# Moving the turned one-hots of a graph attention from VectorE to ScalarE, with the logit sums earlier in TensorE's turn

## The chip, the cores and the metric

The kernel runs on one core of a Trainium2 chip. The metric is the device time of one execution in microseconds; less is better.

## The reference

Four graph layers run one after another on 6250 nodes with 256 features and 100000 edges sorted by destination. The first is two rounds of graph attention with 8 heads; only this part is touched. One round, cut to what matters:

```python
xs = (x @ Ws).reshape(N, H, C)
alpha = a_i[dst] + a_j[src] + edge_terms            # one logit per edge and head
alpha = jnp.where(alpha >= 0, alpha, 0.2 * alpha)
m = jax.ops.segment_max(alpha, dst, num_segments=N)
e = jnp.exp(alpha - m[dst])
s = jax.ops.segment_sum(e, dst, num_segments=N)
msg = xs[src] * (e / (s[dst] + 1e-16))[:, :, None]
out = jax.ops.segment_sum(msg, dst, num_segments=N)
```

## The kernel before

Edges are cut into 832 slots of 128 edges; each slot belongs to one tile of 127 nodes plus a carried row. `phase_attention` runs once for each of the two attention rounds. It handles the slots in 104 groups of 8, one group to a **turn**; four groups stand unrolled in the body of a hardware loop (SETS = 4), so the two rounds make 208 turns. Every engine has its own in-order program, and semaphores tie them together.

What one group g needs, in the order of its data:

- POOL gathers the 8 blocks of 128 source rows (`gather`, line 609) into one of four buffers `x`. The buffer is free when all pair sums of group g-4 are done (line 605).
- SyncE loads `place`, the edges' node positions spread to all partitions, as bf16 (line 624), and `flag` (line 627).
- **The turned one-hot** `fullT` (128 nodes x 8x128 edges, fp32): a 1 where an edge's position equals the partition's number. In the kernel before VectorE makes it with one comparison (`onehotT`, line 826). There is one buffer, so it waits for the logit sums of the group before.
- TensorE's `logit_sums` (lines 660 to 664): edge terms, then 8 small products with `fullT`, then the gathered logits, all into `psA`. ScalarE copies the result to `z` (`copy_logits`, line 751), VectorE makes `al` of it (`leaky`, line 840), TensorE turns `al` (`turn_logits`, line 671), VectorE runs two scans for the running maximum (`scans`, lines 849 and 850), TensorE turns that back (`turn_max`, line 677), VectorE subtracts it (`shifts`, lines 858 and 859), and ScalarE takes the exponentials (`exps`, lines 758 to 760).
- VectorE multiplies the gathered rows by the exponentials, two slots at a time (`messages`, line 866). TensorE sums them by destination with `main`, the unturned one-hot (`pair_sums`, line 684, four pairs of slots, into four PSUM banks `psO`; `main` is made by VectorE's `onehot`, line 831). ScalarE copies the carried row of each slot (`copy_row`, line 765), and VectorE adds the slot's sum to the node table `agg` (`add`, line 875). An add waits for the row's copy; a pair of sums waits for the adds that free its two banks, those of the pair two before it.
- ScalarE also picks the edge terms of group g+3, eight small copies (`pick_terms`, line 742), and copies the gather's indices (`index`, line 732).
- `keep_busy` (line 689) is two matmuls of 512 columns whose result nobody reads.

The order within a turn g is written out by hand on each engine:

```
TensorE: fills, turn_logits(g+1), pair 0, fills, pair 1, fills, turn_max(g+1), pair 2,
         logit_sums(g+2), fills, pair 3
VectorE: leaky(g+1), messages 0, adds 4 5 of g-1, messages 2, adds 6 7 of g-1, scans(g+1),
         tile numbers of g, onehotT(g+2), messages 4, adds 0 1, messages 6, shifts(g+1),
         adds 2 3, onehot(g+1)
ScalarE: pick_terms(g+3), rows 0 to 3, index(g+4), exps(g+1), rows 4 5, copy_logits(g+2), rows 6 7
```

"Tile numbers" (`tiles_of`) are eight register loads on the engine's sequencer; the adds take their address from them.

Of the kernel before, what the change touches and what calls it, by code (L numbers as in the profile page):

```python
# [16 lines left out]
ALU = mybir.AluOpType  # L17
# [507 lines left out]
def phase_attention(nc, m, d, l, sem):  # L525
# [7 lines left out]
    terms_picked = sem("slot_terms_picked")  # L533
    full_ready = sem("onehotT_ready")
# [21 lines left out]
    with ExitStack() as ctx:  # L556
# [9 lines left out]
        row0 = [sb(f"row0{b}", [1, GROUP, AGG]) for b in range(2)]  # L566
        z = sb("z", [P, GROUP, H])
# [31 lines left out]
        with nc.Block() as block:  # L599
# [19 lines left out]
            @block.sync  # L619
            def _(sp):  # L620
                def load_places(g, b):

                    sp.wait_ge(full_ready, g + 1)
                    sp.dma_start(place[b % 2][:], d.places[bass.ds(g * GROUP, GROUP), :].rearrange("(o s) p -> o (s p)", o=1).to_broadcast([P, GROUP * P])).then_inc(loc_ready[b % 2], 16)

                    sp.wait_ge(mT_ready, g + 1)
                    sp.dma_start(flag[b % 2][:, 0:P], d.flags[bass.ds(g * GROUP, GROUP), :, :].rearrange("s h p -> (s h) p")).then_inc(flag_ready[b % 2], 16)

                def store_rows(g, b):
                    sp.wait_ge(copied, g * GROUP + GROUP + BANKS)  # L630
                    sp.dma_start(d.carry[bass.ds(g * GROUP, GROUP), :].rearrange("(o j) k -> o (j k)", o=1),
                                 row0[b][:].rearrange("o j k -> o (j k)")).then_inc(row_stored[b], 16)
                sp.dma_start(terms[:], d.terms[l - 1]).then_inc(terms_ready, 16)
                sp.wait_ge(zeroed, 2)
                for b in range(2):
                    load_places(b, b)
                for b in range(2):
                    load_places(b + 2, b)
                with sp.Fori(0, NG // 2 - 2) as it:
                    for b in range(2):  # L640
                        load_places(it * 2 + b + 4, b)
                        store_rows(it * 2 + b, b)
                for b in range(4):
                    store_rows(NG - 4 + b, b % 2)
                for b in range(2):
                    sp.wait_ge(row_stored[b], 16 * (NG // 2 + 1))

            @block.tensor
            def _(pe):
                regs = [pe.alloc_register(f"pe_n{l}_{j}") for j in range(GROUP)]  # L650
                pe.wait_ge(zeroed, 4)
# [44 lines left out]
                def group(g, b, turn):  # L696
                    g1, b1 = g + 1, (b + 1) % SETS
                    keep_busy()
                    if exists(g1):
                        turn_logits(g1, b1)  # L700
                    pair_sums(g, b, 0)
                    keep_busy()
                    pair_sums(g, b, 1)
                    keep_busy()
                    if exists(g1):
                        turn_max(g1, b1)
                    pair_sums(g, b, 2)
                    if exists(g + 2):
                        logit_sums(g + 2, (b + 2) % SETS, turn + (b + 2) // SETS)
                    keep_busy()  # L710
                    pair_sums(g, b, 3)
# [3 lines left out]
            def _(act):  # L715
                act.sem_inc(copied, BANKS)
                for b in range(2):
                    act.sem_inc(row_stored[b], 16)
# [26 lines left out]

                def copy_logits(g, b):
# [19 lines left out]

                for g in range(2):
                    ts = tiles_of(g)
                    pick_terms(g, g, ts, range(GROUP))
                act.sem_inc(z_ready, 1)  # L770
                copy_logits(0, 0)
                exps(0, 0)
# [4 lines left out]
                def group(g, b, turn):  # L777
                    if exists(g + 3):
# [8 lines left out]
                    if exists(g + SETS):  # L787
                        index(g + SETS, b, turn + 1)
                    if exists(g + 1):
                        exps(g + 1, (b + 1) % SETS)  # L790
                    copy_row(g, b, 4)
                    copy_row(g, b, 5)
                    if exists(g + 2):
                        copy_logits(g + 2, (b + 2) % SETS)
                    copy_row(g, b, 6)
                    copy_row(g, b, 7)
# [6 lines left out]
            def _(dve):  # L803
                regs = [dve.alloc_register(f"dve_n{l}_{j}") for j in range(GROUP)]
                for b in range(2):
# [4 lines left out]
                dve.sem_inc(full_ready, 2)  # L810
# [9 lines left out]

                def onehotT(g, b, pair):
                    dve.wait_ge(loc_ready[b % 2], pair * 16 + 16)

                    if not (isinstance(g, int) and g == 0):
                        dve.wait_ge(ai_ready, g)
                    nc.vector.tensor_scalar(fullT[:].rearrange("p j e -> p (j e)"), place[b % 2][:], m.pidx[:, 0:1], None, ALU.is_equal).then_inc(full_ready, 1)
# [50 lines left out]
                def period(g, b, turn):  # L877
# [12 lines left out]
                    if last_added:  # L890
                        add(g - 1, b0, 6, ns)
                        add(g - 1, b0, 7, ns)
                    if exists(g1):
                        scans(g1, b1, turn * 2 + (b + 1) // 2)
                    ns = tiles_of(g)
                    if exists(g + 2):
                        onehotT(g + 2, b + 2, turn * 2 + (b + 2) // 2)
# [11 lines left out]
                onehotT(0, 0, 0)  # L909
# [4 lines left out]
                onehotT(1, 1, 0)  # L914
# [1819 lines left out]
```

## Time and profile before

| | |
|---|---|
| median of 3 runs | 8941.31 us (8940.38 to 8955.18) |
| the profiled execution | 8943.65 us, span 8942.0 us |
| mean granted TensorE clock | 0.747 of full speed |
| TensorE matmul busy | 6288.6 us (70%) |
| VectorE busy | 4789.7 us (54%) |
| ScalarE busy | 1926.0 us (22%) |
| POOL busy | 4599.6 us (51%) |
| logits copied to `z` (line 751) | 208 times, 104 a round, from 570.8 us to 3616.4 us |

Busy time doesn't count register, branch and semaphore instructions. "PE" is TensorE's matmuls, "PEld" its weight loads, which overlap them; "DVE" is VectorE and "ACT" ScalarE. A matmul in fp32 stands as two instructions in the trace, so one pair of sums is four. The granted clock is a share of full speed: 1.00 is 2.4 GHz and 0.50 is 1.2 GHz. An idle time "<-issue" is one for which the trace shows no semaphore.

### The profile page before, as it was taken

The page shows a single profiled execution, that of the slowest core. Times are in us where ns is not written, and L with a number is a line of the kernel's source. Part 1 is how long each engine was busy: PE and PEld are TensorE (multiplying, and loading weights), DVE is VectorE, ACT ScalarE, POOL GpSimd, SP SyncE. Part 2 cuts the span into 40 slices and gives each one's busy share as a digit, 9 for nine tenths or more (in the row PEclk, how much of TensorE's full clock was granted, in tenths as well). Part 3 has the DMA queues.
Part 4 walks back from the last instruction along what each step waited for, and adds up shares of the span by engine and source line. Part 5 has one row for each costly group of instructions (what it writes and reads, how often), then busy time and mean ns, then how long its engine had stood idle before and what let it go on. Part 6 is the DMA issues. An engine that isn't in the chain of part 4 may idle for free. (4 is left out here: it accounts for less than half of the span.)

```text
span 8942.0 us, 114148 instructions
## 1 busy us (share of the span) xinstructions
PE 6288.6 (70%) x23568; PEld 4316.3 (48%) x23569; DVE 4789.7 (54%) x9732; ACT 1926.0 (22%) x6808; POOL 4599.6 (51%) x4186
## 2 busy tenths in 40 slices
PE   4548899967789999676777778955555666666650
PEld 2236666635566666355666644434444443443330
DVE  4337766666566767675444431134444644444438
ACT  0223333312333333121000011100000222222221
POOL 0036666610466666004777710047777288888880
PEclk7668887777888878675555559977777788888885
DMA  1384444311444434122111123333333366666665
GB/s 38 106 216 112 112 111 111 107 46 56 149 110 112 110 108 115 36 66 62 31 31 30 31 61 133 135 107 104 104 104 104 79 68 68 68 68 68 68 68 175
DMA packets 578153, 801.90 MB, mean 90 GB/s; under 512 B 100092, under 2 KB 453709, under 8 KB 576718
## 3 DMA queue, kind: packets, MB, share of 16 engines
q0 software_dynamic: 269760, 484.09, 27.2%
q1 hardware_dynamic: 281230, 290.19, 10.8%
q10 hardware_dynamic: 27092, 26.85, 1.2%
q8 instruction: 24, 0.39, 0.0%
q14 instruction: 47, 0.39, 0.0%
HBM read 545.48 MB, written 255.28 MB: 90 GB/s over the span
## 5 line engine op out<-in xcount | busy, mean ns | idle before, releaser
L609 POOL DMA_INDIRECT at_x<-table,at_idx x1664 | 1626.2, 977 | 1976.2 <-ACT at_idx L726 1009.1
L2279 POOL DMA_INDIRECT acc<-sc_rows,sc_idx x832 | 1353.3, 1627 | 298.4 <-DMA acc<-sc_rows,sc_idx 185.0
L684 PE MATMUL at_psO<-at_x,at_main 128*128 128x273 f32 x3328 | 1136.7, 471 | 244.9 <-DVE agg L875 240.2
L1679 POOL DMA_INDIRECT rel_x<-rel_table,rel_idx x832 | 793.0, 953 | 963.2 <-DVE rel_sums L1760 710.0
L1679 POOL DMA_INDIRECT conv_x<-conv_table,conv_idx x832 | 808.4, 972 | 767.0 <-DVE conv_msg L1763 513.7
L684 PEld LDWEIGHTS at_psO<-at_x,at_main 128*128 128x128 f32 x3328 | 709.0, 225 | 536.3 <-issue 378.6
L1732 PE MATMUL rel_psO<-rel_x,rel_hot 128*128 128x256 f32 x1664 | 607.6, 544 | 466.6 <-DMA rel_x<-rel_table,rel_idx 394.5
L2319 PE MATMUL sc_psR<-gated,sc_pick 128*128 x1664 | 593.9, 454 | 455.0 <-ACTq L2357 451.2
L875 DVE TENSOR_TENSOR agg<-agg,at_psO 128x273 f32 x1664 | 725.4, 436 | 246.1 <-DVE agg L875 166.5
L1732 PEld LDWEIGHTS rel_psO<-rel_x,rel_hot 128*128 128x128 f32 x1664 | 463.5, 285 | 611.1 <-issue 471.6
L765 ACT COPY at_row<-at_psO 1x273 f32<-1x273 f32 x1664 | 543.0, 374 | 599.7 <-PE at_psO L684 593.5
L2319 PEld LDWEIGHTS sc_psR<-gated,sc_pick 128*128 128x128 f32 x1664 | 297.9, 211 | 750.1 <-issue 741.1
L1797 DVE TENSOR_TENSOR rel_sums<-rel_sums,rel_psO 128x256 f32 x832 | 349.8, 420 | 503.4 <-PE rel_psO L1732 405.6
L689 PE MATMUL at_psK<-at_keep_x,at_keep_w 128*128 128x512 bf16 x1664 | 609.7, 454 | 0.0
L1732 PE MATMUL conv_psO<-conv_msg,conv_hot 128*128 128x65 f32 x1664 | 381.7, 421 | 309.8 <-DVE conv_msg L1786 293.6
L866 DVE TENSOR_TENSOR at_x<-at_x,at_psE 128x512 f32<-128x512 f32 x832 | 566.1, 681 | 1.6 <-issue 1.6
L2355 ACT COPY sc_rows<-sc_psR 128x257 f32<-128x257 f32 x832 | 311.2, 374 | 1114.8 <-POOLq L2278 1090.0
L662 PE MATMUL at_psA<-a_ij,at_fullT 128*128 x3328 | 534.9, 297 | 0.0
L662 PEld LDWEIGHTS at_psA<-a_ij,at_fullT 128*128 128x128 f32 x3328 | 529.1, 249 | 0.0
L1732 PEld LDWEIGHTS conv_psO<-conv_msg,conv_hot 128*128 128x128 f32 x1664 | 362.7, 330 | 328.7 <-issue 328.7
L2422 DVE SCALAR_TENSOR_TENSOR sc_idxf<-sc_count,sc_delta 128x8 f32<-128x8 f32 x105 | 17.6, 167 | 709.2 <-POOLq L2278 708.8
L1716 PE MATMUL conv_psF<-w_radial,conv_attr 12*128 12x64 f32 x1664 | 381.8, 419 | 20.2 <-DMA conv_attr<-in_attr_T 20.2
(412 smaller groups left out, 9192.8 us busy)
## 6 DMA issues: line engine op xcount, KB each, us to landing
at_place<-places SPq DMA_DIRECT2D x208, 256.0 KB
rel_table<-rt_rows SPq DMA_DIRECT2D x50, 1024.0 KB
at_x<-table,at_idx POOLq DMA_INDIRECT x1664
acc<-zeros ACTq DMA_DIRECT2D x4, 6553.5 KB, 63.1
la_t<-acc SPq DMA_DIRECT2D x40, 642.5 KB
conv_attr<-in_attr_T SPq DMA_DIRECT2D x832, 6.0 KB
conv_x<-conv_table,conv_idx POOLq DMA_INDIRECT x832
rel_x<-rel_table,rel_idx POOLq DMA_INDIRECT x832, 2.8
```

What stands on the lines that cost most here:

```text
L609: pool.indirect_dma_start(x[b][:, j, 0:TABW], None, d.table[0:NR, :], bass.IndirectOffsetOnAxis(ap=idx[b][:, j:j + 1], axis=0)).then_inc(x ...
L662: nc.tensor.matmul(psA[:, j, :], fullT[:, j, :], m.a_ij[:, bass.ds(ns[j] * (2 * H) + H, H)], start=False, stop=False, skip_group_check=True)
L684: ins = nc.tensor.matmul(psO[j % BANKS][:, 0:AGG], main[b % 2][:, j, :], x[b][:, j, 0:AGG], start=True, stop=True)
L689: nc.tensor.matmul(psK[:], keep_w[:], keep_x[:], start=True, stop=True)
L765: nc.scalar.copy(row0[b % 2][:, j, :], psO[j % BANKS][0:1, 0:AGG]).then_inc(copied, 1)
L866: nc.vector.tensor_tensor(v, v, psE[:, j:j + 2, :].unsqueeze(3).to_broadcast([P, 2, H, C]), ALU.mult).then_inc(rhs_ready, 1)
L875: nc.vector.tensor_tensor(to, to, psO[j % BANKS][:, 0:AGG], ALU.add).then_inc(acc_done, 1)
L1679: pool.indirect_dma_start(x[b][:, j, 0:WIDE], None, table, bass.IndirectOffsetOnAxis(ap=idx[b][:, j:j + 1], axis=0)).then_inc(x_ready[b], 16)
L1716: ins = nc.tensor.matmul(psF[b % 2][:, j, :], attr[b % 2][:, j, :], m.w_radial[:], start=True, stop=True)
L1732: ins = nc.tensor.matmul(psO[q][j % PER // (PER // 2)][:, j % (PER // 2), :], hot[b % 2][:, j, :], rhs[:, j, :], start=True, stop=True)
L2279: pool.indirect_dma_start(d.acc[k][0:NR + P, :], bass.IndirectOffsetOnAxis(ap=idx[b][:, j:j + 1], axis=0), rows[b % 2][:, j, :], None, com ...
L2319: nc.tensor.matmul(psR[j % 4][:, 0:K], pick[b % 2][:, j, :], m.gated[:, bass.ds(ns[j] * K, K)], start=True, stop=True).then_inc(r_ready, 1)
```

## The change

`onehotT` moves from VectorE to ScalarE, at the head of its turn, and becomes two activations: the distance |place - p| in bf16 (`away`), then relu(1 - distance) into `fullT`. A wait on a semaphore stands between them. `own` holds -p for each partition and is made once per round. On ScalarE `copy_logits(g+2)` moves ahead of `exps(g+1)`, and rows 4 to 7 follow in one piece. On TensorE `turn_logits` moves ahead of the first fills, `logit_sums(g+2)` moves from behind pair 2 to behind pair 1, and one of the four calls of `keep_busy` goes, so that six fills are left of eight. On VectorE the tile numbers are read before the scans instead of behind them.

```diff
 # TensorE
                 def group(g, b, turn):
                     g1, b1 = g + 1, (b + 1) % SETS
-                    keep_busy()
                     if exists(g1):
                         turn_logits(g1, b1)
+                    keep_busy()
                     pair_sums(g, b, 0)
                     keep_busy()
                     pair_sums(g, b, 1)
-                    keep_busy()
+                    if exists(g + 2):
+                        logit_sums(g + 2, (b + 2) % SETS, turn + (b + 2) // SETS)
                     if exists(g1):
                         turn_max(g1, b1)
                     pair_sums(g, b, 2)
-                    if exists(g + 2):
-                        logit_sums(g + 2, (b + 2) % SETS, turn + (b + 2) // SETS)
                     keep_busy()
                     pair_sums(g, b, 3)
 # ScalarE
+                def onehotT(g, b, pair):
+                    act.wait_ge(loc_ready[b % 2], pair * 16 + 16)
+                    nc.scalar.activation(away[:], place[b % 2][:], ACT.Abs, bias=own[:, 0:1]).then_inc(away_ready, 1)
+                    act.wait_ge(away_ready, g + 1)
+
+                    if not (isinstance(g, int) and g == 0):
+                        act.wait_ge(ai_ready, g)
+                    nc.scalar.activation(fullT[:].rearrange("p j e -> p (j e)"), away[:], ACT.Relu, bias=m.ones[:, 0:1], scale=-1.0).then_inc(full_ready, 1)
...
+                act.wait_ge(zeroed, 1)
+                onehotT(0, 0, 0)
...
                 copy_logits(0, 0)
+                onehotT(1, 1, 0)
                 exps(0, 0)
...
                 def group(g, b, turn):
+                    if exists(g + 2):
+                        onehotT(g + 2, b + 2, turn * 2 + (b + 2) // 2)
                     if exists(g + 3):
                         ts = tiles_of(g + 3)
...
                     if exists(g + SETS):
                         index(g + SETS, b, turn + 1)
+                    if exists(g + 2):
+                        copy_logits(g + 2, (b + 2) % SETS)
                     if exists(g + 1):
                         exps(g + 1, (b + 1) % SETS)
-                    copy_row(g, b, 4)
-                    copy_row(g, b, 5)
-                    if exists(g + 2):
-                        copy_logits(g + 2, (b + 2) % SETS)
-                    copy_row(g, b, 6)
-                    copy_row(g, b, 7)
+                    for j in range(4, GROUP):
+                        copy_row(g, b, j)
 # VectorE
+                nc.vector.tensor_scalar(own[:], m.pidx[:], -1.0, None, ALU.mult).then_inc(zeroed, 1)
...
-                def onehotT(g, b, pair):
-                    dve.wait_ge(loc_ready[b % 2], pair * 16 + 16)
-
-                    if not (isinstance(g, int) and g == 0):
-                        dve.wait_ge(ai_ready, g)
-                    nc.vector.tensor_scalar(fullT[:].rearrange("p j e -> p (j e)"), place[b % 2][:], m.pidx[:, 0:1], None, ALU.is_equal).then_inc(full_ready, 1)
...
                         add(g - 1, b0, 7, ns)
+                    ns = tiles_of(g)
                     if exists(g1):
                         scans(g1, b1, turn * 2 + (b + 1) // 2)
-                    ns = tiles_of(g)
-                    if exists(g + 2):
-                        onehotT(g + 2, b + 2, turn * 2 + (b + 2) // 2)
                     messages(g, b, 4)
```

The first marks of `full_ready` come from ScalarE instead of VectorE, and SyncE and TensorE wait for one more mark of `zeroed`.

## Rows read from the trace of the kernel before

**Rows 1.** Busy time by window: the attention phase, one full-clock stretch, one half-clock stretch.
```profile
...
core 0: us, PE busy (x) PEld busy (x) DVE busy (x) ACT busy (x) POOL busy (x), PEclk, DMA share, GB/s
600.00:1650.00 1050.00, 946.66 (x4033) 657.92 (x4034) 735.12 (x1598) 409.77 (x1764) 657.87 (x673) 0.81 0.41 111
1056.00:1067.00 11.00, 9.29 (x48) 6.24 (x48) 8.59 (x20) 4.82 (x21) 8.44 (x9) 1.00 0.51 136
1068.00:1078.00 10.00, 10.00 (x34) 7.45 (x34) 5.32 (x13) 2.46 (x11) 4.13 (x5) 0.50 0.28 80
...
```

**Rows 2.** Waits from 600 to 1650 us: engine, line, cause, total, times, longest.
```profile
...
DVE at_al L840 <- ACT at_z L751: 163.9, 84, 3.8
...
PE at_psO L684 <- DVE agg L875: 101.6, 90, 2.0
...
```

**Rows 3.** Instruction groups from 600 to 1650 us: busy us, mean ns, idle before.
```profile
...
L609 POOL DMA_INDIRECT at_x<-table,at_idx x673 | 658.0, 978 | 392.4 <-issue 200.7 <-PE at_psO L684 191.6
...
L765 ACT COPY at_row<-at_psO 1x273 f32<-1x273 f32 x672 | 219.4, 374 | 233.6 <-PE at_psO L684 231.6
...
L742 ACT COPY at_slot_terms<-at_terms 128x8 f32 x672 | 125.9, 197 | 36.5 <-issue 35.1
...
```

**Rows 4.** Timeline of a full-clock turn: start us, duration us, engine, line, operation.
```profile
...
1056.35 1.18 PE L684 MATMUL at_psO<-at_x,at_main 128*128 128x273 f32 x4 [1.46 <-DVE agg L875]
...
1057.51 0.41 PE L660 MATMUL at_psA<-at_slot_terms,ident 128*128 128x64 f32 x2
...
1058.00 1.22 DVE L831 TENSOR_TENSOR at_main<-at_psT,loc_m 128x1024 f32<-128x1024 f32 x1
...
1059.76 0.59 PE L689 MATMUL at_psK<-at_keep_x,at_keep_w 128*128 128x512 bf16 x2
...
1060.21 0.22 DVE L840 SCALAR_TENSOR_TENSOR at_al<-at_z 128x64 f32<-128x64 f32 x1 [0.99 <-ACT at_z L751]
1060.35 0.68 DVE L866 TENSOR_TENSOR at_x<-at_x,at_psE 128x512 f32<-128x512 f32 x1
...
1060.95 0.43 DVE L875 TENSOR_TENSOR agg<-agg,at_psO 128x273 f32 x1
...
1061.59 0.44 DVE L875 TENSOR_TENSOR agg<-agg,at_psO 128x273 f32 x1 [0.21 <-DVE agg L875]
...
1063.54 0.41 DVE L849 TENSOR_TENSOR_SCAN at_fwd<-at_flag,at_psT 64x128 f32<-64x128 f32 x1
...
1064.68 1.12 POOL L609 DMA_INDIRECT at_x<-table,at_idx  x1 [0.30 <-issue]
...
1064.93 0.75 DVE L826 TENSOR_SCALAR at_fullT<-at_place,pidx 128x1024 f32<-128x1024 bf16 x1 [0.54 <-issue]
...
1065.60 0.68 DVE L866 TENSOR_TENSOR at_x<-at_x,at_psE 128x512 f32<-128x512 f32 x1
...
1067.41 1.90 PE L684 MATMUL at_psO<-at_x,at_main 128*128 128x273 f32 x4 [1.68 <-DVE agg L875]
...
```

**Rows 5.** Timeline of TensorE in the half-clock turn that follows.
```profile
...
1069.10 0.53 PE L660 MATMUL at_psA<-at_slot_terms,ident 128*128 128x64 f32 x2
...
1073.27 1.06 PE L689 MATMUL at_psK<-at_keep_x,at_keep_w 128*128 128x512 bf16 x2
...
1074.12 2.03 PE L684 MATMUL at_psO<-at_x,at_main 128*128 128x273 f32 x4
...
1075.94 1.06 PE L689 MATMUL at_psK<-at_keep_x,at_keep_w 128*128 128x512 bf16 x2
...
1076.93 0.69 PE L671 MATMUL at_psT<-ident,at_al 128*64 128x128 f32 x2
...
```

**Rows 6.** Groups of ScalarE instructions by form, whole span.
```profile
...
L1338 ACT ACTIVATE nm_sq<-agg 128x1280 f32 x20 | 25.5, 1274 | 113.4 <-DVE agg L1381 83.9 <-PE nm_psS L1354 29.5
...
L758 ACT ACT_TABLE_LOAD x1 | 1.3, 1283 | 0.0
...
L1620 ACT ACTIVATE cut_r<-cut_u 128x832 f32<-128x832 f32 x1 | 0.9, 896 | 5.1 <-DVE cut_u L1613 5.1
...
```

More of the change, by code:

```diff
@@ L533, in phase_attention @@
     terms_picked = sem("slot_terms_picked")
+    away_ready = sem("distance_ready")
     full_ready = sem("onehotT_ready")
@@ L566, in phase_attention @@
         row0 = [sb(f"row0{b}", [1, GROUP, AGG]) for b in range(2)]
+        away = sb("away", [P, GROUP * P], BF16)
+        own = sb("own", [P, 1])
         z = sb("z", [P, GROUP, H])
@@ L633, in _ @@
                 sp.dma_start(terms[:], d.terms[l - 1]).then_inc(terms_ready, 16)
-                sp.wait_ge(zeroed, 2)
+                sp.wait_ge(zeroed, 3)
                 for b in range(2):
@@ L650, in _ @@
                 regs = [pe.alloc_register(f"pe_n{l}_{j}") for j in range(GROUP)]
-                pe.wait_ge(zeroed, 4)
+                pe.wait_ge(zeroed, 5)
                 def logit_sums(g, b, turn):
@@ L716, in _ @@
                 act.sem_inc(copied, BANKS)
+                act.sem_inc(full_ready, 2)
                 for b in range(2):
@@ L809, in _ @@
                 nc.vector.tensor_copy(psI, m.iota[:, 0:P]).then_inc(iota_ready, 1)
-                dve.sem_inc(full_ready, 2)
                 dve.sem_inc(mT_ready, 2)
@@ L907, in period @@
                         onehot(g1, b1)
-                onehotT(0, 0, 0)
                 onehot(0, 0)
@@ L913, in _ @@
                 leaky(0, 0)
-                onehotT(1, 1, 0)
                 scans(0, 0, 0)
```

## The prediction

> **What bounds the kernel now.** I read the busy-time windows first, then the waits and groups of the same stretch, then one turn in the timeline. The change touches only the two attention rounds, 208 turns. From 600 to 1650 us POOL issues 673 gathers, eight to a turn, which makes 84.1 turns and 12.48 us a turn [rows 1, 3]. In that stretch TensorE is busy 90% of the time, but its granted clock is 0.81, so it stands at 2.4 GHz for 62% of the time and at 1.2 GHz for 38% [rows 1]. A busy TensorE here is therefore not proof that TensorE is the limit. The waits tell more: VectorE waits for the logits copy 163.9 us (1.95 us a turn), and TensorE waits for VectorE's adds 101.6 us (1.2 us a turn) [rows 2]. Each engine waits for the other once a turn, which is what a closed loop through both looks like.
>
> The timeline shows that loop. Take the full-clock turn from pair 2 to pair 2, 1056.35 to 1067.41, 11.06 us [rows 4]. Pair 2 and the logit sums behind it take 3.4 us (1056.35 to 1059.76), the copy to `z` brings it to `leaky` at 1060.21, and from there VectorE runs messages 0, adds, messages 2, adds, scans, tile numbers, `fullT`, messages 4, adds 0 and 1 without another wait for anybody, 7.20 us, until pair 2 may start. 3.86 + 7.20 = 11.06: the loop explains the full-clock turn whole. The half-clock turns are longer because the same matmuls take longer: the logit sums go from 2.25 us (1057.51 to 1059.76) to 4.17 us (1069.10 to 1073.27) [rows 4, 5]. The clock falls just as TensorE comes out of its 1.68 us stall at 1067.41, when the light logit sums are next. So 11.06 us is the loop, and the other 1.42 us of the mean turn is the price of the clock.
>
> **The change, part by part.**
>
> VectorE. One `fullT` goes, 0.67 us from its start to that of messages 4 (1064.93 to 1065.60). The register loads for the tile numbers stay; their 0.54 us gap [rows 4] now stands ahead of the scans. Take off also the wait at `leaky` (0.99), whose cause moves, and VectorE's own turn is 11.06 - 0.99 - 0.67 = 9.40 us.
>
> The big loop is cut. `logit_sums(g+2)` no longer stands behind pair 2, which waits for adds 0 and 1; its `z` is ready a half turn before VectorE's `leaky` asks for it. What is late next? The tightest chain I find goes through the moved sums to `turn_max`: pair 0, fill and pair 1 start (1.6), pair 1 and logit sums (1.16 + 2.25 = 3.4), `turn_max` (about 0.5, between 0.43 of engine time and the 0.69 us that its sister takes at half clock [rows 5]), then on VectorE shifts, adds 2 and 3, `main` (1.22), `leaky`, messages 0, adds 4 and 5 (4.4 in all), and pair 0 again: 9.9 us at full clock. TensorE alone needs 4 pairs of 1.05, three calls of fills at about 0.5, 2.25 and two turnings of 0.5, 9.0 us.
>
> ScalarE gets two activations of 1024 columns. The trace before has none of that size. The nearest are 896 ns for 832 columns and 1274 ns for 1280 [rows 6], 0.84 ns a column between them, so about 1.06 us each; 0.9 and 1.27 are the bounds. With a gap for the wait between them I take 2.3 us a turn, from 1.9 to 2.7. The Trainium skill ("ScalarE: Activation LUTs", What ACT_TABLE_LOAD costs) puts an activation with a bias pointer at 280 ns + 0.833 ns a column, 1.13 us here; by it the pair would be 2.35 us and the sum the same. The same page (Rules for kernel authors) says to leave relu to VectorE; the row for VectorE's comparison (0.75 us) agrees that ScalarE is about three times slower at this, and what decides is whether ScalarE has the room.
>
> It does, by little. Its path runs: pair 3 ends, rows 6 and 7 (0.7), one-hots (2.3), eight picks at 0.197 (1.6 with a gap), row 0 with its handover (0.55), 5.2 us in all; add 0 may then run, and add 0, add 1, messages 6, shifts, adds 2 and 3 and pair 3 take 4.3 more. 9.5 us, with 9.1 to 9.9 by the bounds. Queued behind the new wait for `away` are the picks (wanted a turn later) and rows 0 to 3, for which VectorE's adds wait; that is the loop just counted. `logit_sums(g+2)` wants `fullT` only behind pair 1, over 1 us after it is there. `place` is loaded about two turns ahead, and is now wanted about a half turn earlier; SyncE's loads wait for `full_ready` as before, so that costs nothing. Moving the copy to `z` ahead of the exponentials costs nothing either: `turn_max` is behind the logit sums in any case.
>
> POOL needs eight gathers and their gaps, (658.0 + 200.7) / 84.1 = 10.21 us a turn [rows 3]. Today that hides in 12.48. Now it is the longest of all at full clock. It may shrink a little, since the gather beside `fullT` took 1.12 us against 0.978 on the mean [rows 3, 4]. I take 10.3 us for a full-clock turn.
>
> The clock. A half-clock turn stays bound by TensorE: four pairs at 1.82, three calls of fills at 0.85 to 0.99, 4.17 and two turnings at 0.62, 15.45 us [rows 5]. How often it comes is the largest unknown. Two fills fewer make TensorE idler. Against that, the 1.7 us stall is gone from ahead of pair 2 and the logit sums, the lightest stretch; behind them now stand `turn_max`, pair 2, fills and pair 3, all dense, where before the sums followed on the stall. The logit sums with `turn_max`, 2.75 us of light work in one piece, can still bring it down, but it should come back sooner. Low never: 10.3 us. Low for 38% as today: 1 / (0.62/10.3 + 0.38/15.45) = 11.8 us. I take 0.4 us for it, a third to a quarter of today's 1.42, hence 10.7 us. The Trainium skill ("TensorE: Matmul & The Clock Gate", What you observe and its table of states) says that idle time lowers the clock and activity releases it; the row of the fall at 1067.41 agrees as far as one row can. By it alone the sum would lie between 10.3 and 11.8 too.
>
> Sum: (12.48 - 10.7) x 206 turns in the steady loop = 367 us. The profiled execution took 8943.65 us, 2.3 above the median of the runs, so the time is 8943.65 - 367, about **8577 us** (8575 against the median). The starts of both rounds change by a few microseconds at most; ScalarE's extra one-hots there stand beside loads.
>
> **The rivals.**
>
> A. The clock stays low as often as today. For it: fills go, and the light stretch stays. Against: the stall goes. 11.8 us a turn, 140 us less: 8800 us.
>
> B. TensorE was the bound after all (90% busy), and the moved waits come back elsewhere. Then the change is worth one call of fills, 0.43 us at full and 0.85 at half clock, 0.6 us a turn with today's clock: 8820 us. Against it: the loop explains 11.06 us to the hundredth.
>
> C. Slower, by the clock: with six fills TensorE is granted half clock more than half the time. At a share s a turn takes 1 / ((1-s)/10.3 + s/15.45); that equals 12.48 at s = 0.52. At 0.6 it is 12.9, 86 us more: 9030 us. For it: TensorE already falls to half clock with eight fills. Against: the stall was part of why.
>
> D. ScalarE changes tables between the distance, the relu and the exponential. One load is 1.283 us [rows 6], two a turn 2.57, and ScalarE's path becomes 12.1 us at full clock and about 12.7 on the mean: 8990 us. Against it: copies and exponentials alternate through all 208 turns with one load in line 758's whole row. The Trainium skill ("ScalarE: Activation LUTs", Table sets) lists abs and relu in the set of the exponential; no row here has an abs, so only the result shows it.
>
> E. The engines pack better than I think: the gathers run in 10.1 us without `fullT` beside them and the clock hardly falls. 10.3 us on the mean: 8495 us.
>
> **How the numbers follow.** The forecast, turns from 10.4 to 11.2 us, 8515 to 8680 us, has 0.56. E and a little beyond: 0.12. A and the values between it and the forecast: 0.15. B: 0.05. C: 0.06. D and other trouble on ScalarE: 0.06. The range from 8480 to 8820 us takes in E, A and B and leaves out C, D and a small tail below. About 0.2% is what a measurement of this kernel can tell from no change. Faster by over 0.2% are the forecast, E, A, B and a small part of D: 0.88. Within it: 0.03. Slower: 0.09.
>
> **What would show it.** Right: turns of about 10.7 us; the wait of `leaky` for the copy to `z` almost gone; ScalarE's two activations near 1.1 us each, its busy time up by about 450 us and no table load among them; VectorE's `fullT` (over 150 us) gone; TensorE's stall ahead of pair 2 gone and a short one ahead of pair 0; POOL's wait for the pair sums down from 2.3 us a turn to a half or less; the granted clock above 0.85. Wrong: a clock of 0.75 or less there (C); table loads in the loop (D); VectorE's adds waiting over 0.5 us a turn for rows 0 and 1 (ScalarE's path longer than counted); TensorE without a stall anywhere and the turn near 12 us (B).

## The result, and the profile after

The changed kernel takes 8477.65 us (median of 4 runs, 8460.66 to 8500.56) against 8940.84 us; the ratio is 0.9484, 95% interval 0.9456 to 0.9512. The forecast was 8577 us, the range 8480 to 8820. The direction was right, the gain was 463 us where 367 were forecast, and the time lies 2 us below the range.

Busy time by window of the changed kernel, the first round and a stretch of the second (against [rows 1]):

```profile
...
core 0: us, PE busy (x) PEld busy (x) DVE busy (x) ACT busy (x) POOL busy (x), PEclk, DMA share, GB/s
600.00:1500.00 900.00, 889.50 (x3980) 623.68 (x4045) 703.51 (x1581) 597.16 (x2023) 671.35 (x704) 0.83 0.50 135
2560.00:2980.00 420.00, 378.98 (x1855) 250.01 (x1884) 331.66 (x737) 278.25 (x943) 313.23 (x328) 0.98 0.50 135
...
```

704 gathers in 900 us are 88.0 turns: **10.23 us a turn**, from 12.48. 328 gathers in 420 us make 10.24 us. (12.48 - 10.23) x 206 is 464 us, the gain between the medians. (The profiled execution, 8500.56 us, is the longest of the four. It is 443 us below the profiled one before, since it spends 16 us more between the two rounds, and 17 us more behind them, where the change touches nothing.) The next thing to see is the clock: 0.83 in the first stretch, 0.98 in the second, and the turn doesn't change. In the first TensorE stands at half clock for a third of the time and is busy 99%, and the turn is the same length.

The groups of the first stretch (against [rows 3]):

```profile
...
L612 POOL DMA_INDIRECT at_x<-table,at_idx x704 | 672.6, 955 | 229.0 <-issue 225.0 <-PE at_psO L687 4.0
...
L777 ACT COPY at_row<-at_psO 1x273 f32<-1x273 f32 x704 | 221.7, 373 | 209.7 <-PE at_psO L687 209.7
...
L756 ACT ACTIVATE at_fullT<-at_away,ones 128x1024 f32<-128x1024 bf16 x88 | 101.0, 1148 | 4.6
L751 ACT ACTIVATE at_away<-at_place,at_own 128x1024 bf16<-128x1024 bf16 x88 | 100.6, 1143 | 0.0
...
```

The two activations take 1.143 and 1.148 us, 2.29 together, where 2.3 was taken from the bounds; no table load is in the loop (line 770 has one in the whole span, as line 758 had before). The gather is 0.955 us instead of 0.978.

The waits of the same stretch (against [rows 2]):

```profile
...
DVE agg L883 <- ACT at_row L777: 71.5, 165, 0.9
...
POOL at_x L612 <- PE at_psO L687: 4.0, 13, 0.3
...
PE at_psO L687 <- DVE agg L883: 0.2, 1, 0.2
...
```

VectorE's wait for the logits copy (163.9 us before) isn't in the list any more, and TensorE's wait for the adds went from 101.6 to 0.2 us. POOL's wait for the pair sums, 191.6 us before [rows 3], is 4.0 us. New is VectorE's wait for ScalarE's rows, 71.5 us in 88 turns, 0.8 us a turn. Its place is plain in the timeline of one turn of the changed kernel:

```profile
...
1003.38 1.14 ACT L751 ACTIVATE at_away<-at_place,at_own 128x1024 bf16<-128x1024 bf16 x1
...
1004.55 1.15 ACT L756 ACTIVATE at_fullT<-at_away,ones 128x1024 f32<-128x1024 bf16 x1
...
1005.61 1.41 ACT L745 COPY at_slot_terms<-at_terms 128x8 f32 x8
...
1006.93 1.21 ACT L777 COPY at_row<-at_psO 1x273 f32<-1x273 f32 x4
...
1007.53 0.44 DVE L883 TENSOR_TENSOR agg<-agg,at_psO 128x273 f32 x1 [0.66 <-ACT at_row L777]
...
1008.18 0.44 DVE L883 TENSOR_TENSOR agg<-agg,at_psO 128x273 f32 x1 [0.21 <-ACT at_row L777]
...
1008.77 2.19 PE L687 MATMUL at_psO<-at_x,at_main 128*128 128x273 f32 x4
...
1010.75 1.06 PE L692 MATMUL at_psK<-at_keep_x,at_keep_w 128*128 128x512 bf16 x2
...
1011.60 1.38 PE L687 MATMUL at_psO<-at_x,at_main 128*128 128x273 f32 x4
...
1013.01 0.66 ACT L777 COPY at_row<-at_psO 1x273 f32<-1x273 f32 x2 [1.37 <-PE at_psO L687]
...
1013.57 1.14 ACT L751 ACTIVATE at_away<-at_place,at_own 128x1024 bf16<-128x1024 bf16 x1
...
```

ScalarE makes the two one-hots from 1003.38, the picks from 1005.61, and rows 0 to 3 only from 1006.93; VectorE's add has waited 0.66 us for the first of them, and its second add waits too; pair 2 starts at 1008.77, 0.15 us behind that add's end, and runs at half clock (2.19 us instead of 1.19 at full), fills and pair 3 follow without a stall, then rows 6 and 7 at 1013.01, which have waited for pair 3, and the next one-hots at 1013.57, 10.19 us after the last. Anything that is done once a turn comes back after one turn; what makes this a ring that is as long as the turn is that no step of it has slack beyond a handover. TensorE has no stall in this stretch either, so its own work, at this clock, is as long too.

### The profile page after: what moved, and what is told of

Read it like the earlier page. It is cut to its first block and busy times, and to the rows that moved or that the text cites. A ratio compares the mean times of both kernels' runs of the same rounds, so it can differ in the third digit from the quotient of the medians.

```text
span 8498.9 us, 113470 instructions
## 1 busy us (share of the span) xinstructions
PE 6023.3 (71%) x22996; PEld 4125.2 (49%) x23153; DVE 4643.8 (55%) x9526; ACT 2325.1 (27%) x7224; POOL 4572.7 (54%) x4186
## 5 line engine op out<-in xcount | busy, mean ns | idle before, releaser
L612 POOL DMA_INDIRECT at_x<-table,at_idx x1664 | 1591.0, 956 | 1559.9 <-ACT at_idx L729 1009.2
L777 ACT COPY at_row<-at_psO 1x273 f32<-1x273 f32 x1664 | 524.6, 373 | 454.4 <-PE at_psO L687 454.1
L692 PE MATMUL at_psK<-at_keep_x,at_keep_w 128*128 128x512 bf16 x1092 | 401.3, 442 | 20.5 <-issue 16.1
L665 PE MATMUL at_psA<-a_ij,at_fullT 128*128 x3328 | 402.4, 256 | 0.0
L665 PEld LDWEIGHTS at_psA<-a_ij,at_fullT 128*128 128x128 f32 x3328 | 395.0, 195 | 0.0
```

What stands on the lines that cost most here:

```text
L612: pool.indirect_dma_start(x[b][:, j, 0:TABW], None, d.table[0:NR, :], bass.IndirectOffsetOnAxis(ap=idx[b][:, j:j + 1], axis=0)).then_inc(x ...
L665: nc.tensor.matmul(psA[:, j, :], fullT[:, j, :], m.a_ij[:, bass.ds(ns[j] * (2 * H) + H, H)], start=False, stop=False, skip_group_check=True)
L692: nc.tensor.matmul(psK[:], keep_w[:], keep_x[:], start=True, stop=True)
L777: nc.scalar.copy(row0[b % 2][:, j, :], psO[j % BANKS][0:1, 0:AGG]).then_inc(copied, 1)
```

## The experiments

Fourteen kernels ran, each timed in three rounds against the kernel before on the same chip. In the expectations, theory P says that POOL's gathers set the turn, V and C a chain through VectorE and TensorE, S the ring through ScalarE just shown, T TensorE's own work; L and W are told where they stand. The kernels with seven gathers leave out the load of every eighth slot's rows, so they compute other messages; they only show what POOL's time is worth. Medians of different kernels, taken in different rounds, are compared by their ratios to the kernel before, which itself moved between 8925 and 8942 us.

| run | what it is | median us | ratio to before, 95% interval |
|---|---|---|---|
| changed kernel | | 8477.65 | 0.9484 (0.9456 to 0.9512) |
| e1 | new order only, one-hot on VectorE | 8737.65 | 0.9765 (0.9735 to 0.9796) |
| e2 | one-hots on ScalarE only | 9059.34 | 1.0134 (1.0112 to 1.0157) |
| e3 | changed, seven gathers | 8463.9 | 0.9472 (0.9448 to 0.9495) |
| e4 | changed, eight fills | 8573.51 | 0.9578 (0.9553 to 0.9603) |
| e5 | new order, one-hot early on VectorE | 8470.97 | 0.9495 (0.9475 to 0.9515) |
| e6 | changed, fourth call of fills behind pair 2 | 8564.64 | 0.9595 (0.9579 to 0.9611) |
| e8 | before, six fills | 9018.46 | 1.0109 (1.0088 to 1.0129) |
| e9 | e2, picks later | 8607.27 | 0.9637 (0.9618 to 0.9656) |
| e10 | changed, picks later | 8448.93 | 0.9463 (0.9439 to 0.9488) |
| e11 | e6, picks later | 8480.13 | 0.9497 (0.9473 to 0.9521) |
| e12 | e10, seven gathers | 8460.0 | 0.9466 (0.9434 to 0.9499) |
| e13 | e5, seven gathers | 8456.57 | 0.9472 (0.9447 to 0.9498) |
| e14 | e12, fills moved | 8497.98 | 0.9507 (0.9484 to 0.9531) |
| e15 | e10, fills moved | 8511.25 | 0.9521 (0.9493 to 0.9548) |

### The two halves of the change, each alone

**e1_order_only.** The kernel before, with the changed kernel's order on TensorE (six fills) and of the copies on ScalarE. `onehotT` stays on VectorE, behind the scans.

> The kernel before with only the new order: on TensorE the logit sums behind pair 1 and six fills, on ScalarE the logits copy ahead of the exponentials; the turned one-hot stays on VectorE behind the scans. Theory P (POOL's eight gathers, 10.2 us a turn, set the turn of the changed kernel): VectorE's own turn is then 9.40 + 0.67 = 10.1 us, still just under POOL's, so nearly the whole gain is here: 10.3 to 10.5 us a turn, 8480 to 8530 us. Rival V (a chain through VectorE sets the turn): the 0.67 us come back in full, 10.9 us a turn, 8615 us.

8738 us, less than half of the gain, and slower than either theory had it (8530 and 8615). The waits of this kernel, 700 to 1500 us, name the reason:

```profile
...
PEld at_psA L660 <- DVE at_fullT L823: 78.3, 69, 1.6
...
PE at_psA L660 <- DVE at_fullT L823: 48.5, 68, 1.2
...
```

126.8 us in 69 turns, 1.8 us a turn: the logit sums had moved ahead, but the one-hot they read had not. It was still made behind the scans.

**e2_scalar_only.** The changed kernel with the old order on TensorE (eight fills) and the old order of the copies on ScalarE.

> The changed kernel with the old order on TensorE (logit sums behind pair 2, eight fills) and of the copies on ScalarE; only the one-hots are on ScalarE. The loop through pair 2 is left whole: 11.06 - 0.67 = 10.39 us at full clock, and the clock still falls about as often. Theory P: 11.8 us a turn, 8800 us, a third of the gain. Rival (the one-hots' place is what counts, the order is not): 8480 to 8550 us.

9059 us, slower than before, and no theory had said so. Timeline of this kernel ahead of pair 2:

```profile
...
901.16 1.41 ACT L746 COPY at_slot_terms<-at_terms 128x8 f32 x8
...
902.47 1.20 ACT L778 COPY at_row<-at_psO 1x273 f32<-1x273 f32 x4
...
903.07 0.44 DVE L886 TENSOR_TENSOR agg<-agg,at_psO 128x273 f32 x1 [1.03 <-ACT at_row L778]
...
904.29 1.34 PE L687 MATMUL at_psO<-at_x,at_main 128*128 128x273 f32 x4 [1.82 <-DVE agg L886]
...
```

Picks, rows, add (1.03 us of waiting), pair 2 (1.82 us of waiting). In the old order the logit sums stand behind pair 2, so the one-hots' 2.3 us were put onto the loop through pair 2, by way of ScalarE's rows. The expectation had taken 0.67 us off that loop and forgotten the way around.

**e9_scalar_only_picks_later.** Tests just that: e2 with the picks behind rows 0 to 3.

```diff
                 def group(g, b, turn):
                     if exists(g + 2):
                         onehotT(g + 2, b + 2, turn * 2 + (b + 2) // 2)
-                    if exists(g + 3):
-                        ts = tiles_of(g + 3)
-                        act.wait_ge(ai_ready, g + 2)
-                        pick_terms(g + 3, b + 3, ts, range(GROUP))
                     act.wait_ge(row_stored[b % 2], turn * 32 + (b // 2) * 16 + 16)
                     for j in range(4):
                         copy_row(g, b, j)
+                    if exists(g + 3):
+                        ts = tiles_of(g + 3)
+                        act.wait_ge(ai_ready, g + 2)
+                        pick_terms(g + 3, b + 3, ts, range(GROUP))
```

> The one-hots-only kernel (old order, eight fills) with ScalarE's eight picks of edge terms moved behind rows 0 to 3. Theory S (the one-hots delay rows 0 and 1, for which VectorE's adds and with them pair 2 and the logit sums wait): the picks' 1.6 us come off that path, which falls below the loop through pair 2, and the turn is 11.8 us or less, 8720 to 8810 us. Rival (the loss came from the clock or from TensorE, which the picks don't touch): 9040 to 9070 us as without the move.

8607 us: about 450 us back from moving eight small copies behind four others. The explanation holds (from 600 to 1500 us VectorE's adds waited for ScalarE's rows 106.1 us in e2, 25.8 us here), and more came back than expected (8720 to 8810); the granted clock of that stretch is 0.88 here and 0.78 in e2. This run also says how much of the gain doesn't need the new order. It has the old order and eight fills, its loop through pair 2 is uncut (VectorE still waits for the logits copy 104.2 us in 81 turns, 1.3 us a turn), and it is 3.6% faster than the kernel before, where the whole change is 5.2% faster. Taking the comparison off VectorE's part of the loop is worth that much once the picks are out of the way (their move alone wasn't tried on the kernel before); the same eight fills and picks with the new order (e11, below) are 5.0% faster.

**e5_vector_early.** e1 with the one-hot made earlier, still by one comparison on VectorE:

```diff
                     if last_added:
                         add(g - 1, b0, 6, ns)
                         add(g - 1, b0, 7, ns)
+                    if exists(g + 2):
+                        onehotT(g + 2, b + 2, turn * 2 + (b + 2) // 2)
+                    ns = tiles_of(g)
                     if exists(g1):
                         scans(g1, b1, turn * 2 + (b + 1) // 2)
-                    ns = tiles_of(g)
-                    if exists(g + 2):
-                        onehotT(g + 2, b + 2, turn * 2 + (b + 2) // 2)
```

> The new order with six fills as in the order-only kernel, the one-hot still one comparison on VectorE, but ahead of the tile numbers and the scans instead of behind them. In the order-only kernel TensorE waited 1.8 us a turn for that one-hot ahead of the logit sums. Theory L (what cost there was lateness, not VectorE's time): VectorE's own turn is 10.1 us, so 10.3 to 10.6 us a turn, 8480 to 8550 us. Rival W (VectorE's time counts in full on the chain that sets the turn): 10.23 + 0.67 = 10.9 us or more, 8620 us.

8471 us, 9 below theory L's band, with an interval that overlaps the changed kernel's. So the 260 us between e1 and the changed kernel were lateness. In the new order the move to ScalarE did one useful thing, to make the one-hot early; VectorE can do that as well. Whether it can in the old order too wasn't tried.

### What the turn of 10.23 us hangs on

**e3_seven_gathers.** POOL takes one gather less a group (and the counts of three waits follow):

```diff
-                    for j in range(GROUP):
+                    for j in range(GROUP - 1 if reused else GROUP):
                         pool.indirect_dma_start(x[b][:, j, 0:TABW], None, d.table[0:NR, :],
```

> The changed kernel with seven gathers a group instead of eight behind the first four groups; the eighth slot's rows are left as they are, so its messages are not the reference's. Theory P: POOL's share falls from 10.2 to 9.0 us a turn and the turn falls to the next bound, the chain through turn_max of 9.9 us or TensorE with its half-clock stretches: 9.8 to 10.1 us, 8400 to 8450 us, with POOL waiting for the pair sums about 1 us a turn. Rival V (another chain sets the turn, POOL only keeps up): 8470 to 8485 us, nothing gained.

8464 us, above theory P's band (8400 to 8450) and 6 us below V's; the intervals of this and the changed kernel overlap. The window of the first round in this kernel:

```profile
...
600.00:1500.00 900.00, 819.06 (x4047) 536.36 (x4047) 711.25 (x1584) 596.23 (x2022) 586.62 (x616) 0.98 0.45 122
...
```

616 gathers at seven a turn are 88.0 turns in 900 us again, though POOL now waits for the pair sums 1.6 us a turn (123.8 us in 78 turns, 700 to 1500 us). So POOL is not what holds the turn alone: theory P, as the expectation had it, falls. The clock is 0.98 in this stretch of this kernel and 0.83 from 2560 to 2980 us, where 288 gathers make 41.1 turns in 420 us: the same turn at both clocks again, with the two stretches changed about.

**e4_eight_fills.** The fourth call back, between the logit sums and `turn_max`:

```diff
                         logit_sums(g + 2, (b + 2) % SETS, turn + (b + 2) // SETS)
+                    keep_busy()
                     if exists(g1):
                         turn_max(g1, b1)
```

> The changed kernel with the fourth call of fills back, between the logit sums and turn_max. Theory P: TensorE's slack takes it, or the clock rises by it; 10.2 to 10.3 us a turn, 8475 to 8495 us. Rival T (TensorE, busy 99% of the first round, sets the turn): 0.43 to 0.6 us a turn more, 8565 to 8600 us.

8574 us, the time that T said, but not by T's cause. The timeline of this kernel in a full-clock turn:

```profile
...
1200.49 1.18 PE L687 MATMUL at_psO<-at_x,at_main 128*128 128x273 f32 x4
...
1203.88 0.59 PE L692 MATMUL at_psK<-at_keep_x,at_keep_w 128*128 128x512 bf16 x2
...
1204.96 0.22 DVE L867 TENSOR_TENSOR at_shifted<-at_al,at_psT 128x64 f32<-128x64 f32 x1 [1.00 <-PE at_psT L680]
...
1209.47 1.18 PE L687 MATMUL at_psO<-at_x,at_main 128*128 128x273 f32 x4 [0.71 <-DVE agg L884]
...
1211.07 1.19 PE L687 MATMUL at_psO<-at_x,at_main 128*128 128x273 f32 x4
...
```

From pair 1 to pair 1 it is 10.58 us. TensorE isn't at its limit here: it stalls 0.71 us ahead of pair 0. The added fills (1203.88) stand ahead of `turn_max`, and VectorE waits for that 1.00 us. So the fills lengthened the chain through `turn_max`, which the prediction put at 9.9 us, by about their own 0.4 us.

**e6_fills_behind_pair2** puts the fourth call behind pair 2, off the chain through `turn_max`:

```diff
                     pair_sums(g, b, 2)
                     keep_busy()
+                    keep_busy()
                     pair_sums(g, b, 3)
```

> The changed kernel with eight fills, the fourth call next to the one ahead of pair 3 instead of ahead of turn_max. Theory C (a chain that runs from the logit sums through turn_max and the shifts sets the turn, and the fourth call lay on it): here it lies beside the chain, the time stays within 15 us of 8478. Rival T (TensorE's own work sets the turn): as dear as ahead of turn_max, 8550 to 8600 us.

8565 us, T's band again. But the waits of this kernel, 700 to 1500 us, hold another reading:

```profile
...
DVE agg L884 <- ACT at_row L778: 80.2, 125, 1.2
...
```

1.1 us a turn, more than the 0.8 of the changed kernel. The fills behind pair 2 lie on ScalarE's ring (pair 2, fills, pair 3, rows 6 and 7, one-hots, picks, row 0, adds, pair 2). If the ring made them dear, they are cheap once it is shorter: **e11_eight_fills_picks_later**, e6 with the picks moved as in e9.

> The changed kernel with eight fills (the fourth call behind pair 2, which cost 87 us) and the picks behind rows 0 to 3. Theory S (that call was dear because it lies on the ring rows 6 and 7, one-hots, picks, row 0, adds, pair 2, fills, pair 3): with the picks off the ring the time is back at 8460 to 8500 us. Rival T (TensorE's own work with its half-clock stretches): still 8540 to 8570 us.

8480 us, inside theory S's band: the picks' move alone, with the same work on TensorE, gives back 84 us. So T falls as the whole cause for that place, and the ring is shown. It isn't all of it, as e10 (next) says: with the picks moved in both, the fourth call still costs 31 us (8480 against 8449; the slowest of e10's four executions is below the fastest of e11's), and 0.13 us a turn (695 gathers from 600 to 1500 us, 10.36 us, against 704). What these 31 us hang on wasn't looked for.

**e10_picks_later.** The changed kernel with only the picks moved.

> The changed kernel with ScalarE's eight picks moved behind rows 0 to 3. Theory P (POOL's gathers set its turn, the ring through ScalarE is only just as long): POOL's bare pace is 10.1 us, so at most 0.1 us a turn comes back, 8450 to 8478 us. Rival S (ScalarE's ring sets the turn): up to the chain through turn_max, 9.9 us, 8400 to 8420 us.

8449 us, the lowest median of all and 1 us below P's band; its interval overlaps the changed kernel's, so it is not told apart from it. Its window, 600 to 1500 us:

```profile
...
600.00:1500.00 900.00, 812.83 (x3981) 536.15 (x4045) 712.08 (x1583) 619.52 (x2024) 671.38 (x704) 0.98 0.49 136
...
```

The clock is 0.98 here and 0.83 in the changed kernel, and the count of gathers is 704 in both: the same turn to the gather. (That the move of the picks raised the clock isn't shown: over the whole span three of the changed kernel's four executions have 0.785 or 0.786, like this kernel's 0.782 to 0.786; only the profiled one has 0.756.) The ring through ScalarE and the half clock of the first round cost the changed kernel nothing there, since something else has the same length. The timeline of this kernel shows what:

```profile
...
1205.12 1.19 PE L687 MATMUL at_psO<-at_x,at_main 128*128 128x273 f32 x4
...
1208.62 0.43 PE L680 MATMUL at_psT<-ident,at_mx 64*128 64x64 f32 x2
...
1209.18 0.22 DVE L866 TENSOR_TENSOR at_shifted<-at_al,at_psT 128x64 f32<-128x64 f32 x1 [0.53 <-PE at_psT L680]
...
1213.68 1.18 PE L687 MATMUL at_psO<-at_x,at_main 128*128 128x273 f32 x4 [0.70 <-DVE agg L883]
...
1215.28 1.18 PE L687 MATMUL at_psO<-at_x,at_main 128*128 128x273 f32 x4
...
```

It is the prediction's chain through `turn_max`: pair 1 and logit sums 3.50 us, `turn_max` 0.56, VectorE from the shifts until pair 0 may start 4.50, pair 0 and fills 1.60, 10.16 us where 9.9 were counted.

**e12_seven_picks_later** takes POOL and the ring off together, **e13_seven_vector_early** takes POOL off e5.

> The changed kernel with the picks behind rows 0 to 3 and seven gathers a group instead of eight (the eighth slot's rows are left as they are, so its messages are not the reference's). With POOL at 9 us and ScalarE's ring shorter by 1.6 us, the chain through turn_max (9.9 us at full clock) is next: 9.9 to 10.1 us a turn, 8410 to 8450 us, if POOL and ScalarE's ring held the turn together. Rival T (TensorE with a third of the turn at half clock holds it): 8460 to 8480 us.

> The kernel with the one-hot early on VectorE (8471 us), with seven gathers a group (the eighth slot's messages are not the reference's). Theory P (POOL alone sets its turn; VectorE needs 10.1 us itself): 0 to 0.1 us a turn less, 8450 to 8470 us. If VectorE's time were far from the limit: 8410 us as with the one-hots on ScalarE.

8460 and 8457 us. Neither falls against its own kernel with eight gathers by more than the intervals. The second is as expected; the first missed (8410 to 8450): what its expectation called next, at 9.9 us, is there already, and is 10.16. **e14_seven_fill_moved** was meant to shorten it by the fills, and **e15_fill_moved** is the same with eight gathers:

```diff
                     pair_sums(g, b, 0)
-                    keep_busy()
                     pair_sums(g, b, 1)
...
                     pair_sums(g, b, 2)
                     keep_busy()
+                    keep_busy()
                     pair_sums(g, b, 3)
```

> The kernel with seven gathers and the picks behind rows 0 to 3 (8460 us), with the fills between pair 0 and pair 1 moved behind pair 2, next to the others there; six fills stay, and the eighth slot's messages are not the reference's. Theory C (what is left at 10.13 us a turn is the chain pair 0, fills, pair 1, logit sums, turn_max, shifts, adds, main, leaky, messages, adds): 0.3 to 0.45 us a turn less, 8370 to 8400 us, unless pair 1 waits for adds 6 and 7 instead, which stand 0.15 us behind it. If no such chain holds it: 8450 to 8470 us.

> The same move of the fills with all eight gathers, picks behind rows 0 to 3 (without the move 8449 us). Theory P (POOL's bare pace, 10.06 us a turn, is the next bound): 0.05 to 0.1 us a turn less, 8425 to 8445 us. If POOL is no bound: 8370 to 8400 us as with seven gathers.

8498 and 8511 us, both outside what was expected; e15 is clearly slower than e10, e14's interval overlaps e12's. The clock from 600 to 1500 us fell to 0.91 and 0.90, from 0.98. The chain itself didn't get shorter, and the timeline of e14 in a full-clock turn shows why:

```profile
...
1212.04 0.44 DVE L883 TENSOR_TENSOR agg<-agg,at_psO 128x273 f32 x1 [0.21 <-DVE agg L883]
...
1212.61 1.19 PE L687 MATMUL at_psO<-at_x,at_main 128*128 128x273 f32 x4 [0.41 <-DVE agg L883]
...
1213.76 0.41 PE L663 MATMUL at_psA<-at_slot_terms,ident 128*128 128x64 f32 x2
...
1216.11 0.43 PE L680 MATMUL at_psT<-ident,at_mx 64*128 64x64 f32 x2
...
1216.67 0.22 DVE L866 TENSOR_TENSOR at_shifted<-at_al,at_psT 128x64 f32<-128x64 f32 x1 [0.52 <-PE at_psT L680]
...
1217.09 0.44 DVE L883 TENSOR_TENSOR agg<-agg,at_psO 128x273 f32 x1
...
1218.10 1.22 DVE L839 TENSOR_TENSOR at_main<-at_psT,loc_m 128x1024 f32<-128x1024 f32 x1
...
1219.23 0.21 DVE L848 SCALAR_TENSOR_TENSOR at_al<-at_z 128x64 f32<-128x64 f32 x1
1219.36 0.68 DVE L874 TENSOR_TENSOR at_x<-at_x,at_psE 128x512 f32<-128x512 f32 x1
...
1219.96 0.43 DVE L883 TENSOR_TENSOR agg<-agg,at_psO 128x273 f32 x1
...
1220.96 0.68 DVE L874 TENSOR_TENSOR at_x<-at_x,at_psE 128x512 f32<-128x512 f32 x1
...
1222.20 0.44 DVE L883 TENSOR_TENSOR agg<-agg,at_psO 128x273 f32 x1 [0.21 <-DVE agg L883]
...
```

Pair 1 (1212.61) waits for add 7 (1212.04 + 0.44), not for the fills. From there: logit sums 1213.76, `turn_max` 1216.11, shifts 1216.67 (VectorE had waited 0.52 us), add 2 1217.09, `main` 1218.10, `leaky`, messages 0, adds 4 and 5, messages 2, adds 6 and 7 at 1222.20: 10.16 us, with no slack in it but the handovers. The exception that e14's expectation named is the case. With the fills gone from between pairs 0 and 1, adds 6 and 7 hold pair 1 at the same place: the chain has two first legs of one length, and 10.16 us by either.

**e8_old_order_six_fills.** The kernel before with one edit:

```diff
                     pair_sums(g, b, 1)
-                    keep_busy()
                     if exists(g1):
                         turn_max(g1, b1)
```

> The kernel before with one call of fills less (the one ahead of turn_max), nothing else. In the old order that call lies beside the loop through pair 2, where TensorE waits for VectorE anyway. Theory C: nothing gained at full clock, and the clock falls more, 8940 to 9050 us. Rival T (TensorE's work counts): 0.5 us a turn less, 8830 us.

9018 us, 1.1% more than before, as C said. Its window, 600 to 1650 us:

```profile
...
600.00:1650.00 1050.00, 914.48 (x3627) 664.29 (x3687) 703.66 (x1527) 390.70 (x1686) 629.76 (x643) 0.76 0.39 106
...
```

643 gathers instead of 673, at a clock of 0.76 instead of 0.81 [rows 1]. The two matmuls that nobody reads were worth 0.6 us a turn to the kernel before, in this stretch (13.06 against 12.48), and 0.5 by the ratio. The changed kernel has six fills as well; what two more would be worth there is e4 and e6, a loss.

## Why the prediction came out as it did

**The loop through pair 2** was read rightly: cut, it took both waits of [rows 2] with it. But it isn't the only way to most of the gain: e9 has 3.6 of the 5.2% with the loop uncut. POOL's pace (10.21 us forecast, 10.20 measured), the activations (2.3 against 2.29) and the absence of table loads came out as written. VectorE's own turn was put a little low, 9.40 us; in the turn of e14 it is 9.64 (10.16 less the 0.52 that it waited). ScalarE's busy time rose by 399 us (1926.0 to 2325.1) where 450 were forecast. Rival D and rival C did not happen; B's six fills had no gain of their own.

**The step that failed is the clock's term**: "I take 0.4 us for it, a third to a quarter of today's 1.42, hence 10.7 us." It measured nothing: 10.23 us a turn with the clock at 0.83 and at 0.98. The mistake was in the kind of mean. The prediction mixed whole turns at full clock (10.3) with whole turns bound by TensorE at half clock (15.45). But the half clock came in pieces shorter than a turn, in the same place each turn (pair 2, fills, part of pair 3). TensorE is busy 9.2 us of the turn in the second window above (378.98 us in 41 turns, clock 0.98) and 10.1 us in the first (889.50 in 88, clock 0.83). The half clock added 0.9 us of busy time and found 1.0 us idle; the turn had the room. By the prediction's own full-clock figure, 10.3 us, the sum would have been 8495 us, and by POOL's 10.21 us, 8476. That this figure was so near is in part luck. It was taken from POOL as the longest at full clock; the runs with seven gathers have the same turn, and the chain that was counted as shorter, 9.9 us, takes 10.16. Rival E said the same time, with 0.12, and for another reason (that the clock would hardly fall and the gathers would run in 10.1 us).

The room was nearly used up: a fourth call of fills cost half a microsecond a turn in e4 and e6. In e4 that was the chain through `turn_max`; in e6 it was for the most part the ring, as e11 showed, and 0.13 us a turn is left open.

**What sets 10.23 us** is not one thing. With seven gathers the turn stays (e3, e12), so POOL alone doesn't hold it. In e10 and e12 the clock is near full, ScalarE's ring is 1.3 us shorter (the picks, 1005.61 to 1006.93 above), and the turn is the chain through `turn_max`, 10.16 us in the turns shown; e4 lengthened that chain and the turn grew with it. The mean is a little longer, 10.23; what the rest of it is wasn't looked for. With eight gathers POOL's own pace, (672.6 + 225.0) / 88 = 10.20 us in the groups above, is the same length within 0.05 us. Whether it would hold the turn if that chain were shorter wasn't shown: no run shortened the chain. In the half-clock stretch of the changed kernel TensorE's own work (10.1 us) and ScalarE's ring (10.19 us) are as long as well.

**The credit was given wrongly.** The prediction took 0.67 us a turn off VectorE for the move to ScalarE. e5 keeps that time on VectorE and is as fast, because in the new order the time isn't on what sets the turn; in the old order, where it is, e9 shows that it counts. And "What is late next?" was answered for the whole change only: the ring through ScalarE was reckoned at 9.5 us and read as harmless. Together with the half clock behind pair 2 it was as long as the turn (10.19 us in the timeline above), and in the old order it made the same move a loss (e2). The prediction's own sign against that reading, adds waiting over 0.5 us a turn for rows, came true in the first round (0.8 us).

## What to carry to other kernels

When an operation moves earlier, look at when its inputs are made before crediting the engine that makes them: here the new order made the kernel 2.4% faster without its one-hot early (e1), and 5.0% with it, still on VectorE (e5). When half clock comes in pieces shorter than a turn, charge it first against the slack of the engine that it slows, not as a mean over turns. And before adding work ahead of an engine's short copies, follow them around: eight copies of 0.2 us, moved behind four others, were worth about 450 us (e9 against e2) or nothing that could be told from noise (e10), according to whether the ring through them was the longest.

## What the runs showed of the hardware

- TensorE's granted clock goes with the order of the work and not only with its amount: six fills gave 0.76 in the old order (e8; eight gave 0.81) and 0.83 to 0.98 in the new; moving one call of fills from between pairs 0 and 1 to behind pair 2 took it from 0.98 to 0.90 (e10, e15). One kernel has both: 0.83 and 0.98 in the two stretches of the changed kernel, 0.98 and 0.83 in those of e3.
- A ScalarE activation of 128 x 1024 with a pointer for its bias took 1.143 us to bf16 and 1.148 us to fp32. The prediction's interpolation, 1.06 us, was 0.09 low. The Trainium skill ("ScalarE: Activation LUTs", What ACT_TABLE_LOAD costs) gives 1.13 us, which the trace bears out. Abs, relu and exp took turns through 208 turns with one table load. The Trainium skill ("ScalarE: Activation LUTs", Table sets) lists abs and relu in the set of exp; the trace agrees.
- With the comparison of bf16 on VectorE gone, POOL's gathers took 0.955 us on the mean instead of 0.978. In e5, where it stays, the mean is 0.974 (685.73 us for 704 gathers). Over all kernels here the mean from 600 to 1500 us is 0.974 to 0.988 us where VectorE makes that comparison (before, e1, e5, e8, e13) and 0.953 to 0.958 where it doesn't. That one slows the other is likely from this; no run took the comparison away with nothing in its place.
